# Channel mixing on x by a transposed product on TensorE, and the wide product in two column groups of 512 beside a gate group

## The reference

```python
h = gelu(gelu(cond_128 @ W0 + b0) @ W1 + b1)
att = softmax(h @ W2 + b2)                                  # (32, 8)
agg_w = einsum('bk,koi->boi', att, weight); agg_b = att @ bias_k
y = einsum('boi,bih->boh', agg_w, x) + agg_b[:, :, None]    # channel mixing
xf = y.reshape(2048, 1024)
gate = softmax(xf @ gate_W.T); w = top-2 of gate, normalised, 0 elsewhere
lora = ((xf @ A) * w * 2.0) @ B
out = x + xf @ W_base.T + lora
```

## Time and profile before

| what | value |
|---|---|
| median of three timed runs | 267.35 us (266.09 to 267.67) |
| the profiled execution (its span; the page gives no other time of it) | 265.7 us |
| what lies between that span and the median | 1.65 us |
| TensorE busy (matmul / weight load) | 254.0 us (96%) / 247.9 us (93%) |
| VectorE, ScalarE, GpSimd busy | 141.1, 69.0, 65.2 us |
| matmul instructions, weight loads | 1451, 1451 |
| mean granted TensorE clock | 0.981 |

### The profile page before, as it was taken

The page is one execution under the profiler, slowest core; times in us unless marked ns, Lnnn a source line. Parts: engine busy times, 40 slices in busy tenths (PEclk is TensorE's granted clock), DMA queues, the critical chain, the costliest instruction groups (busy, mean ns, idle before and its releaser), DMA issues.

```text
span 265.7 us, 4272 instructions
## 1 busy us (share of the span) xinstructions
PE 254.0 (96%) x1451; PEld 247.9 (93%) x1451; DVE 141.1 (53%) x398; ACT 69.0 (26%) x156; POOL 65.2 (25%) x46
## 2 busy tenths in 40 slices
PE   8699679999999999999999999999999999999994
PEld 5498678999999999999999999999999999999993
DVE  2998999446536345434445363454344453634542
ACT  4539034131313122131213131221312231311110
POOL 3657688030210303040302103040304021030000
PEclk9999795999999999999999999999999999999999
DMA  6998020042423060606042240606060332404012
GB/s 199 400 379 286 0 79 1 0 160 96 144 97 140 15 222 1 237 0 216 21 150 86 79 158 9 228 0 237 0 205 32 129 108 74 163 18 142 0 79 79
DMA packets 9527, 31.02 MB, mean 117 GB/s; under 512 B 1072, under 2 KB 1584, under 8 KB 9520
## 3 DMA queue, kind: packets, MB, share of 16 engines
q1 hardware_dynamic: 9520, 30.93, 33.3%
HBM read 22.54 MB, written 8.39 MB: 116 GB/s over the span
## 4 chain that ended last, share of the span: by engine, by line
PE 85%; DVE 9%; DMA 2%; ACT 2%; SPq 1%; issue 1%; DVEq 0%; ACTq 0%
PE z_ps L660 23%; PE z_ps L662 23%; PE z_ps L661 23%; PE o_ps L679 3%; DVE w_lo L455 3%; PE o_ps L690 3%; PE o_ps L688 3%; PE o_ps L676 3%; PE o_ps L674 3%; DMA w_raw<-wext_in 2%; DVE b_lo L607 1%; ACT w_hi L335 1%; DVE blk_lo L467 1%; DVE gate L509 1%; DVE lora_split L517 1%; DVE att_rep L569 1%
## 5 line engine op out<-in xcount | busy, mean ns | idle before, releaser
L660 PE MATMUL z_ps<-w_hi,xt_hi 128*128 128x366 f32 (+1 forms) x384 | 130.8, 341 | 4.1 <-DVE w_lo L455 4.0
L662 PE MATMUL z_ps<-w_hi,xt_lo 128*128 128x366 f32 (+1 forms) x384 | 129.1, 336 | 0.0
L661 PE MATMUL z_ps<-w_lo,xt_hi 128*128 128x366 f32 (+1 forms) x384 | 128.9, 336 | 0.0
L660 PEld LDWEIGHTS z_ps<-w_hi,xt_hi 128*128 128x128 f32 x384 | 74.4, 194 | 6.0 <-DVE w_lo L455 5.0
L460 DVE TENSOR_TENSOR z_lo<-z_ps,z_hi 128x366 fp32r<-128x366 f32 (+1 forms) x48 | 25.8, 538 | 96.4 <-ACT z_hi L341 96.3
L296 POOL TENSOR_TENSOR xt_lo<-xt_raw,xt_hi 128x1024 fp32r<-128x1024 f32 x14 | 36.8, 2628 | 154.3 <-ACT xt_hi L331 154.3
L661 PEld LDWEIGHTS z_ps<-w_lo,xt_hi 128*128 128x128 f32 x384 | 74.6, 194 | 0.0
L662 PEld LDWEIGHTS z_ps<-w_hi,xt_lo 128*128 128x128 f32 x384 | 74.2, 193 | 0.0
L341 ACT ACTIVATE z_hi<-z_ps 128x366 fp32r<-128x366 f32 (+1 forms) x48 | 22.8, 475 | 149.9 <-PE z_ps L662 149.8
L476 DVE SCALAR_TENSOR_TENSOR x_nat<-w_sum,bias,x_nat 128x1024 f32<-128x1024 f32 (+2 forms) x18 | 23.0, 1280 | 3.8 <-DMA x_nat<-x_in 3.8
L531 DVE TENSOR_TENSOR out_sb<-o_ps,x_nat 128x366 f32<-128x366 f32 (+1 forms) x44 | 19.9, 505 | 4.7 <-PE o_ps L690 3.8
(11 more groups left out here) (94 smaller groups left out, 170.0 us busy)
## 6 DMA issues: line engine op xcount, KB each, us to landing
x_nat<-x_in SPq DMA_DIRECT2D x16, 512.0 KB, 4.6
xt_raw<-xt_in SPq DMA_DIRECT2D x15, 512.0 KB, 5.1
out<-out_sb SPq DMA_DIRECT2D x15, 512.0 KB, 3.0
w_raw<-wext_in SPq DMA_DIRECT2D x8, 366.0 KB, 8.7
w_raw<-wext_in SPq DMA_DIRECT2D x4, 364.0 KB, 5.8
par<-small_in SPq DMA_DIRECT2D x1, 576.0 KB, 7.4
xt_raw<-xt_in SPq DMA_DIRECT2D x2, 256.0 KB, 4.2
out_sb<-bt_in SPq DMA_DIRECT2D x2, 256.0 KB, 12.3
```

The lines of the kernel that those rows point to most:

```text
L660: nc.tensor.matmul(dst, hi, w_cols(w_hi, g, k), start=(k == 0), stop=False)
L661: nc.tensor.matmul(dst, hi, w_cols(w_lo, g, k), start=False, stop=False)
L662: last = nc.tensor.matmul(dst, lo, w_cols(w_hi, g, k), start=False, stop=(k == KC - 1))
```

## The change

Mixing is moved in front of the product. x is loaded as it lies in memory (128 tokens by 1024 features). `y_group` makes y transposed on TensorE: for each of the 8 chunks of 128 features the stationary operand is x's chunk and the moving operand the mixing matrix, 3 matmuls of 128 columns per chunk, 24 per tile. VectorE adds the bias (`y_bias`), which is laid out along the tokens by 4 matmuls of 512 columns at the start; ScalarE and VectorE split y (`y_high`, `y_low`). `gate_group` computes gate and A columns: weight high and low parts lie side by side, so per chunk there is one matmul of 144 columns (y high) and one of 72 (y low), 16 per tile. `z_group` computes W_base's 1024 columns in two groups of 512, 8 chunks by 3 matmuls each, 48 per tile, and its PSUM banks are double buffered over tiles. LoRA is 4 matmuls of 512 columns into the same banks. Row sums, the mixing of z and its evacuation are gone. The prologue no longer starts with products: tile 0 needs the mixing matrix first, and weights are split in 8 pieces of 1024 columns instead of 12 of 728 or 732. `gating` has 14 operations.

```diff
-        z_ps = [ps(f"z_ps{g}") for g in range(G)]
-        o_ps = [ps(f"o_ps{g}") for g in range(G)]
+        z_ps = [[ps(f"z_ps{q}{h}") for h in range(2)] for q in range(2)]
+        y_ps = [ps(f"y_ps{h}") for h in range(2)]
...
             sp.dma_start(par[:, 0:C_MLP], small[:, 0:C_MLP]).then_inc(mlp_loaded, 16)
+            sp.dma_start(par[:, C_MLP:C_ALL], small[:, C_MLP:C_ALL]).then_inc(par_loaded, 16)
+            load_xr(0, 0)
+            sp.dma_start(g_raw[:, :, :].rearrange("p k c -> p (k c)"), gq).then_inc(g_loaded, 16)
             for n in range(PIECES):
...
+            x_low(0, 0)
+            pool.wait_ge(att_step, 4)
+            pool.wait_ge(par_loaded, 16)
+            for n in range(BIAS_PARTS):
+                bias_product(n)
+            x_low(1, 1)
...
+            def step(j, parity, y_next=True, x_next=True):
+                t = 2 * j + parity
+                ratio_exp(t)
+                lora_copy(t)
+                if y_next:
+                    y_high(t + 1, 1 - parity)
+                if x_next:
+                    x_high(j + 1, parity)
+                    block_high(t + 2, parity)
...
+            def y_bias(t, first=False):
+                for h in range(2):
+                    dve.wait_ge(y_mm, 2 * t + h + 1)
...
+                    nc.vector.tensor_tensor(y32[:, half(h)].rearrange("p (k c) -> p k c", c=P),
+                                            y_ps[h][:, :].rearrange("p (k c) -> p k c", c=P),
+                                            bias[:, None, cols].to_broadcast([P, HC, P]),
+                                            ALU.add).then_inc(y_ready, 1)
...
-                z_low(t - 1, 2)
-                x_bias(j, parity)
-                z_low(t, 0)
-                block_low(t, parity)
                 add_out(j - 1 + parity, 1 - parity, first=early)
...
+                gating(t)
+                if y_next:
+                    y_bias(t + 1)
+                    y_low(t + 1, 1 - parity)
+                if x_next:
+                    block_low(t + 2, parity)
...
+            w_low(0)
+            dve.wait_ge(g_hi_ready, 1)
...
+            block_low(0, 0)
+            w_low(1)
+            dve.wait_ge(bias_ready, 1)
+            y_bias(0, first=True)
+            block_low(1, 1)
+            y_low(0, 0)
+            for n in range(2, PER_H + 2):
                 w_low(n)
...
+            gating(0, first=True)
+            for n in range(PER_H + 2, PIECES):
                 w_low(n)
...
+            def gate_group(t, parity, first=False):
+                pe.wait_ge(y_lo_ready, 2 * t + 2)
...
+                for k in range(KC):
+                    nc.tensor.matmul(g_ps[:, 0:GW], chunk(y_hi, parity, k), g_w[:, k, :],
+                                     start=(k == 0), stop=False)
+                    last = nc.tensor.matmul(g_ps[:, 0:GZ], chunk(y_lo, parity, k), g_w[:, k, 0:GZ],
+                                            start=False, stop=(k == KC - 1))
...
+                    nc.tensor.matmul(dst, chunk(y_hi, parity, k), w_cols(w_hi, h, k), start=(k == 0), stop=False)
+                    nc.tensor.matmul(dst, chunk(y_hi, parity, k), w_cols(w_lo, h, k), start=False, stop=False)
+                    nc.tensor.matmul(dst, chunk(y_lo, parity, k), w_cols(w_hi, h, k), start=False, stop=False)
+
+            def y_group(t, parity, first=False):
+                pe.wait_ge(x_lo_ready, t + 1)
+                pe.wait_ge(blk_lo_ready, 2 * (t + 1))
+                for h in range(2):
+                    if not first:
+                        pe.wait_ge(y_ready, 2 * (t - 1) + h + 1)
+                    for k in range(HC * h, HC * (h + 1)):
+                        dst = y_ps[h][:, (k - HC * h) * P:(k - HC * h + 1) * P]
+                        nc.tensor.matmul(dst, chunk(x_hi, parity, k), blk_hi[:, parity, :], start=True, stop=False)
+                        nc.tensor.matmul(dst, chunk(x_hi, parity, k), blk_lo[:, parity, :], start=False, stop=False)
+                        mm = nc.tensor.matmul(dst, chunk(x_lo, parity, k), blk_hi[:, parity, :],
+                                              start=False, stop=True)
...
+            def step(j, parity, y_next=True):
                 t = 2 * j + parity
...
+                gate_group(t, parity)
                 z_group(t, parity, 0)
...
+                transpose_lora(t)
+                if y_next:
+                    y_group(t + 1, 1 - parity)
                 z_group(t, parity, 1)
...
+                lora_groups(t, parity)
```

More of the change, by code:

```diff
@@ L226, in _ @@
[L226 to L233, removed]
+                sp.dma_start(piece(w_raw, n), piece(wq, n)).then_inc(w_loaded[n], 16)
+                if n == PER_H - 1:
+                    load_xr(1, 1)
@@ L234, in _, with step @@
+            for s in range(2):
+                sp.dma_start(b_raw[s * ER:(s + 1) * ER, :], bt).then_inc(bt_loaded, 16)
             load_xn(0, 0)
             load_xn(1, 1)
[L238 to L242, removed]
+            def step(j, parity, more=True, store=True):
                 t = 2 * j + parity
[L245 to L256, removed]
+                if more:
+                    sp.wait_ge(x_lo_ready, t + 1)
+                    load_xr(t + 2, parity)
+                if store:
+                    sp.wait_ge(evacuated, 2 * t)
+                    sp.dma_start(out_t[t - 1], out_sb[:, 1 - parity, :]).then_inc(out_stored[1 - parity], 16)
+                    if more or parity == 0:
+                        load_xn(t + 1, 1 - parity)
@@ L257, in _ @@
+            step(0, 0, store=False)
+            step(0, 1)
+            with sp.Fori(1, PAIRS - 1) as j:
                 step(j, 0)
                 step(j, 1)
[L259 to L265, removed]
+            step(PAIRS - 1, 0, more=False)
@@ L481, in gating, with y_low @@
+            def y_low(t, parity):
+                for h in range(2):
+                    dve.wait_ge(y_hi_ready, 2 * t + h + 1)
+                    nc.vector.tensor_tensor(y_lo[:, parity, half(h)], y32[:, half(h)],
+                                            y_hi[:, parity, half(h)].bitcast(F32),
+                                            ALU.subtract).then_inc(y_lo_ready, 1)
+            def gating(t, first=False):
                 base = GATE_STEPS * t
-                dve.wait_ge(o_done, G * t + 1)
@@ L695, in transpose_lora, with lora_groups @@
+            def lora_groups(t, parity):
+                pe.wait_ge(lora_t_ready, t + 1)
+                for h in range(2):
+                    dst = z_ps[parity][h][:, :]
+                    nc.tensor.matmul(dst, lora_t[:, :], b_hi[:, half(h)], start=False, stop=False)
+                    nc.tensor.matmul(dst, lora_t[:, :], b_lo[:, half(h)], start=False,
+                                     stop=True).then_inc(main_done, 1)
+            def transpose_lora(t, first=False):
                 pe.wait_ge(gate_step, GATE_STEPS * (t + 1))
+                if not first:
+                    pe.wait_ge(lora_t_ready, t)
```

581 lines of the change are left out of this document (207 added, 374 removed).

## The result

The changed kernel is slower, as forecast: median 296.88 us (293.04 to 299.48, six executions) against 267.51 us for the kernel before on the same chip (265.76 to 269.27, six). The forecast was 297.5, and the profiled execution has the very span of the sum, 295.8 us. That agreement is partly luck: two terms were off by 5 us each, in opposite directions.

A forecast was written before the change was run, and what follows sets the result against it. TensorE's matmul stream was taken as the bound: 42.8 us to step 1, plus 251.6 for 15 steps of 16.77, less 2.7, plus 1.2 and 2.93, gives 295.8; with 1.65 to the timed median, 297.5 us, range 284 to 312.

The forecast's parts named there:

- The bound: Whole kernel: TensorE's matmul stream sets the time, other engines hide behind it; a tile goes from 14.64 to 16.77 us.
- Narrow matmuls: Mixing and gate group: each matmul costs its weight load, 0.111 us; 2.66 and 1.78 us a tile.
- second rival: Narrow matmuls: loads overlap in part, 0.085 us each; a tile 15.7 us, total 281; chance 0.07.
- the first (columns only): All matmuls: narrow ones cost their columns, wide ones columns plus 15 ns; a tile 14.25 us, total 257; chance 0.04.
- Wide matmuls: Wide product and LoRA: 512 columns cost 235 ns by columns; 11.28 and 0.94 us a tile.
- The start: Before the steady steps: tile 0 waits for the mixing matrices; step 1 begins at 42.8 us, bounds 39 and 50.
- forecast hole of 2.5 us before tile 0's transpose: Start: TensorE stands 2.5 us, as tile 0's gating, queued on VectorE behind four weight pieces, ends at 33.4.
- step 1 far from 43 us: Start: step 1 beginning far from 43 us would show the prediction wrong.
- third rival: Steps: each `y_group` brings a 3.4 us fall to half clock, 1.7 us more a tile, total 325; chance 0.08.
- What hides beside TensorE: Steps: gating, bias and split of y stay hidden; VectorE's work about 7.5 us a tile in a 16.8 us step.
- The range: Total: wide -5 to +2.5 us, narrow -3 to +3, start -4 to +7, 286 to 310; widened to 284 to 312.

The follow-up runs named there:

- e1: Changed kernel with mixing's operands exchanged, the mixing matrix stationary: 6 matmuls of 512 columns a tile instead of 24 of 128; 272.75 us, ratio 1.021 to the kernel before.
- e2: Changed kernel without the low part of the gate weights in 7 of 8 chunks, still 16 gate matmuls; 298.23 us, ratio 1.116 to the kernel before.
- e3: Changed kernel with each wide matmul of 512 columns cut in two of 256; 305.18 us, ratio 1.141 to the kernel before.
- e4: Changed kernel with filling matmuls in front of tile 0's mixing and between the bias matmuls; 296.86 us, ratio 1.113 to the kernel before.
- e8: Changed kernel with filling matmuls around tile 0's mixing and three of four bias groups moved between tile 0's wide matmuls; 295.31 us, ratio 1.103 to the kernel before.
- e5: Changed kernel with gate columns back in the wide product, groups of 364, 366 and 366, no gate group; 281.97 us, ratio 1.057 to the kernel before.
- e6: Kernel before with column groups of 76, 510 and 510 instead of 364, 366 and 366; 303.95 us, ratio 1.140.

## Why the prediction was right, and where it was not

**The bound.** Right. TensorE's stream sets the time, the kernel lost 1.8 us a tile in it, and no wait took part: from 40 to 285 us there is no hole.

**Narrow matmuls.** Right, and the core of the case. 24 x 0.111 = 2.66 was 2.68; 16 x 0.111 = 1.78 was 1.71. e1 and e2 show the cause apart from the rest: same columns in fewer loads gain 1.32 us a tile, fewer columns under as many loads gain nothing. The second rival (loads half hidden, 85 ns) and the first (columns only) both fail on the 0.112 us from start to start. The Trainium skill, page TensorE: Matmul & The Clock Gate, section Back-to-back issue gap, gives about 81 ns for a sustained stream of 128 columns; here it is 112, and the measurement decides.

**Wide matmuls.** The term that was mis-sized: 235 ns by columns, where the other reckoning in the same sentence, a fixed 15 ns, gave 229 and was the right one. 227 to 230 ns were measured, and e3 shows that the loss is per matmul. I had chosen by the 292 columns of the earlier trace rows, whose starts are given to 0.01 us; at that size the two reckonings differ by less. 52 wide matmuls make the tile 16.45 instead of 16.77, and 15 steps 4.8 us less than forecast.

**The start.** Also mis-sized, the other way: step 1 at 47.96 instead of 42.8. The rows of PE in the start of the changed kernel:

```profile
16.78 0.41 PE L567 MATMUL y_ps<-blk_lo,x_hi 128*128 128x128 f32 x1
17.00 0.41 PE L568 MATMUL y_ps<-blk_hi,x_lo 128*128 128x128 f32 x1
...
21.82 5.49 PE L607 MATMUL z_ps<-bias_in,ones 8*128 8x512 f32 x6
27.23 0.49 PE L541 MATMUL g_ps<-g_w,y_hi 128*128 128x144 f32 x1
...
30.67 0.77 PE L554 MATMUL z_ps<-w_hi,y_hi 128*128 128x512 f32 x1
...
47.96 0.23 PE L541 MATMUL g_ps<-g_w,y_hi 128*128 128x144 f32 x1
```

`y_group(0)` began at 16.54, 1.3 us before the forecast, mainly since the two `att_diag` operations took 0.60 instead of 2.65. It then ran at half clock, 0.21 us a matmul: 2.4 us more. Between it and the gate group stand six more bias matmuls (three groups of two passes), 5.5 us; I had counted one of the four bias groups, and 3.0 us of waiting on VectorE there: 2.5 more. Gate group and first group of 512 took 11.6 us instead of 7.4: 4.1 more, at half clock up to 36.1. The forecast hole of 2.5 us before tile 0's transpose did not come, because TensorE was so late that gating, done at 37.4, was ready. Together -1.3 + 2.4 + 2.5 + 4.1 - 2.5 = 5.2. So what failed in the start's term is the clock, which I had at 1.2 GHz only for the 16 mixing-matrix matmuls, though the earlier trace rows show the fall in the start of the kernel before, and the count of bias groups. One of the prediction's own signs of being wrong, step 1 far from 43 us, came true. Start and end together, the span less 16 tiles, were to fall from 31.5 to 27.5 us and came to 32.6.

That the half clock as such costs 5 us is not shown: e4 and e8 lifted most of it, without a gain that can be told. In e8 VectorE's order, and in its profile the late `att_diag`, took its place. Among the six executions of the changed kernel the longest span, 297.8, has the mean clock 0.999, the shortest, 291.3, 0.988. What makes them differ by 6.5 us stays open. One thing that changes from profile to profile is `att_diag`: it took 0.60 us in the four (the changed kernel, e2, e3, e4) where GpSimd's `x_low` began 0.34 us or more behind it, and 2.76 to 3.28 in the three (e1, e5, e8) where `x_low` began 0.25 us behind it or ahead of it. But e5's profile, with 3.28, is of its shortest execution, so this alone does not explain the difference.

**The clock in the steps, third rival.** Refuted. Each `y_group` is 2.7 us of matmuls under one load's time, and the granted clock stays at 1.00 from 40 to 285 us.

**What hides beside TensorE.** Right: gating, bias and split of y never showed. The page has no wait of the gate group for VectorE in the steps, at 127.22 / 14.9 = 8.5 us of VectorE's work a tile, where I had reckoned 7.5.

**The range.** Both errors lay inside the bounds given (start -4 to +7, wide -5 to +2.5), and nearly cancelled.

## What to carry to other kernels

Price a stream of matmuls by its count as well as by its columns: here each costs its columns plus 14 ns, and never less than a load, 112 ns, which by these two numbers is what some 235 columns take ((112 - 14) x 2.4, an estimate: no run has a width between 144 and 256). Equal middling groups (364, 366, 366) therefore, in e5 and e6, beat two full ones and a narrow one, and an operand that must be stationary in 128-column portions makes mixing 1.3 us a tile dearer than the same columns under few loads. Before chasing a low clock in a start, see whether another engine is late there; and look at what GpSimd runs beside short VectorE operations on the critical chain.

## What was not expected of the hardware

The granted clock was 0.50 from 15.6 to 36.1 us although TensorE was busy for 19.79 of 20.40 us; the matmuls in it were narrow, or used 8 of 128 rows, up to 30.7 us. In the steps, narrow stretches of 1.7 and 2.7 us between full ones left it at 1.00.

An operation of 8 columns on VectorE takes 0.23 us alone and 1.71 beside GpSimd, and one wait on GpSimd, off the critical path, makes the kernel before 1.7% faster.
